# GpSimd adds a fourth tile of gathered rows in a graph kernel; TensorE's products in one run; the last normalisation earlier

## The chip, the cores and the metric

The kernel runs on one core of a Trainium2 chip. The metric is the device time of one execution in microseconds (us), the median of the runs. A core has TensorE (PE in the profile, its weight loads PEld), VectorE (DVE), ScalarE (ACT), GpSimd (POOL) and SyncE (SP), each with its own instruction stream; they wait for each other through semaphores.

## What is computed

Two graph layers over 6250 nodes of 128 features and 100000 edges, each with a residual and a layernorm:

```python
# layer 0 (e: 100000 x 128, fc_w: 512 x 128, attn: 100 x 4 x 128)
f = (e @ fc_w.T).reshape(-1, 4, 128)
w = attn[rel]
feat = sum(leaky_relu(w * f, 0.2), axis=1)
msg = h[src] + feat
x = layernorm(x + segment_sum(msg, dst))
# layer 1
h = x @ W.T + b
s1 = h @ a1_w + a1_b;  s2 = h @ a2_w + a2_b
e = leaky_relu(s1[src] + s2[dst], 0.01)
att = softmax of e over the edges of each src
x = layernorm(x + segment_sum(att * h[dst], src))
```

## The kernel before, in words

The edges are sorted by dst. **Stage 1** (layer 0) takes them in `G0` = 196 groups of 512 edges, four tiles (`TG`) of 128. Per group g, with the engine and the name of the helper:

- SP loads the 512 edge rows (`e_sb`) and relation numbers.
- GpSimd's `group(g)` issues four indirect DMAs (L523), one per tile, which gather the rows x[src] of the group into slot g % 4 of `xg` (printed as `room`). Then `scatter(g - 3)` issues one indirect DMA (L534) that writes sorted edge records. Before the gathers it waits until the slot is free (`agg_done`).
- TensorE's `products(g, u)`, u = 0 to 3: the edge tile times `fc_sb` into FP[u // 2] (L845, float32, two matmul records), and the one-hot relation times the two parts of attn into WP[u % 2] (L854, two records). `aggregate(g - 2)` sums the messages into a 64-column window of nodes: L864 multiplies the four message tiles `msg` with the one-hot `doh`, and L866 multiplies the gathered x rows of the fourth tile with the same `doh` into the same accumulation. `compact(g)` (L877) makes the sorted edge records.
- ScalarE's `step(g)`: `blocks` (L638, `boh`), `copy 0` (L631, WP to `w_sb`), `window_gap` (L648), `copy 1`, `relation` of g + 1 (L618, L623), `copy 2`, `window` (L657, makes `doh`; it overwrites the `doh` of g - 2, so it waits for `agg_done` of g - 2), `copy 3`, `compact` (L665).
- VectorE's `group(g)`: `records` (L1159, `joh`), `weigh_pair` 0 (L1178, z = FP x w_sb for tiles 0 and 1), `halve` and `finish` of g - 1 (L1193 `hs`, L1201 `msg`), `weigh_pair` 1 (L1178, tiles 2 and 3), `accumulate` of g - 2 (L1169, adds AP to `accT`), `add_x` of g - 1 (L1209: adds the x rows of three tiles, `X_DVE` = 3, to `msg`), `slope` (L1185, y = max(0.2 z, z), 2048 elements per partition).

`weigh_pair` 1 of g waits for `copy 3` of g, which stands behind `window` of g on ScalarE. `msg`, `doh`, `joh` have two buffers, `xg` four. FP[0] and FP[1] are each free again when their `weigh_pair` is done.

**Between the stages** the first layernorm and h = x W are computed block by block (52 blocks of 122 nodes).

**Stage 2** (layer 1) takes the edges, now sorted by src block, in at least 200 groups (208 here). GpSimd gathers four tiles of h rows per group (L567, L575); the other engines compute a running softmax sum per block. Once all edges of a block are in, the block is averaged, its residual added, and it is normalised. In the last 16 groups VectorE's `early(j)` does average, residual and statistics of two blocks per group, for blocks 0 to 31 (L1457, L1463, L1468). After the last group (`update`, L1341) come `average`, statistics and `normalise` of the other blocks in runs of 8, 8 and 4, and the normalisation of all 52 (ScalarE L795, VectorE L1517). SP and GpSimd store the output in chunks of eight blocks.

Of the kernel before, what the change touches and what calls it, by code (L numbers as in the profile page):

```python
# [26 lines left out]
EARLY = 32  # L27
RUNS = [(0, EARLY)] + [c for c in CHUNKS if c[0] >= EARLY]
BY_DVE = [q for q in range(NS) if (q % 4 == 3 if q < EARLY else q % 2 == 1)]
# [41 lines left out]
def build(nc, x, x_t, e, src_pg, dst_pg, dst_g, rel_g, fcT, attn, WT, Wn, b, a1, a1b, a2, a2b, out):  # L71
    with ExitStack() as ctx:
# [192 lines left out]
        def sums_of(k):  # L265
# [46 lines left out]
        x_added = sem("x_added")  # L312
        r_done = sem("r_done")
# [23 lines left out]
                     boh_ready, joh_ready, x_added, r_done, r_copied)  # L337
# [51 lines left out]
        n_avg = sem("n_avg")  # L389
        n_stat = sem("n_stat")  # L390
# [122 lines left out]
        def _(pool):  # L513
# [23 lines left out]
            with pool.Fori(0, pass_count(pool)) as p:  # L537
# [4 lines left out]
                for g in range(SLOTS, G0):  # L542
                    group(g, g % SLOTS, False)
                    scatter(g - RLAG, (g - RLAG) % SLOTS, False)
                for j in range(RLAG, 0, -1):
                    scatter(G0 - j, SLOTS - j, False)
                for k in range(SLOTS):
# [51 lines left out]
        def _(act):  # L599
# [173 lines left out]
            with act.Fori(G1_LEAST - 2 * S1, act.snap(more + (G1_LEAST - 2 * S1 + 1)), S1) as i:  # L773
                for k in range(S1):
                    idx(i + k + AHEAD, (k + AHEAD) % S1)
                    block_s1(i + k + AHEAD, (k + AHEAD) % S1, False)
                    step1(i + k, k, False)
            for k in range(S1):
# [3 lines left out]
                step1(tail + k, k, False, k < S1 - 2)  # L782
            for k in range(S1 - 2, S1):
# [4 lines left out]

            for c, (q0, q1) in enumerate(RUNS):
                run = slice(q0, q1)  # L790
                act.wait_ge(n_var, c + 1)
                nc.scalar.activation(rstd[:, run], mv[:, run, 1], ACT.Sqrt, bias=eps_col[0:BN, :]).then_inc(n_std, 1)
                act.wait_ge(n_rs, c + 1)
                for q in [q for q in BY_ACT if q0 <= q < q1]:
                    nc.scalar.activation(xn[:, q, :], xn[:, q, :], ACT.Identity, bias=nmr[:, q:q + 1],  # L795
                                         scale=rstd[:, q:q + 1]).then_inc(fin_act, 1)
# [3 lines left out]
        def _(pe):  # L800
# [185 lines left out]
        def _(dve):  # L986
# [225 lines left out]
            def group(g, k, lead):  # L1212
# [13 lines left out]
            with dve.Fori(0, pass_count(dve)) as p:  # L1226
                for k in range(SLOTS):
                    group(k, k, True)
                for g in range(SLOTS, G0):
                    group(g, g % SLOTS, False)  # L1230
# [219 lines left out]
            def early(j):  # L1450

                if j == 0:
                    dve.wait_ge(st_ready, tail - LAG + 1)
                    weights(0, EARLY)
                if j < S1 * 2:
                    for q in (2 * j, 2 * j + 1):
                        ins = v.scalar_tensor_tensor(xn[:, q, :], o_sb[:, q, 0:P], rstd[:, q:q + 1], xn[:, q, :],  # L1457
# [107 lines left out]
```

## Time and profile before

| | |
|---|---|
| median of 3 runs | 2639.86 us (2639.47 to 2640.49) |
| the profiled execution's own time | 2640.72 us |
| its span | 2638.9 us |
| PE busy | 2162.6 us (82%) |
| DVE busy | 2244.4 us (85%) |
| ACT busy | 1724.0 us (65%) |
| POOL busy | 1914.7 us (73%) |
| stage 1, about | 85 to 1500 us |
| stage 2, about | 1547 to 2608 us, then the end of the last normalisation |

The span is what the engines' records cover; the execution's own time is 1.8 us more. Busy time leaves out semaphore waits, and also the time that GpSimd spends in issuing between two indirect DMAs. Records of one engine may overlap by up to 0.1 us, since an instruction may begin while the one before it still writes; the pace of an engine is therefore read from one start to the next.

### The profile page before, as it was taken

What the parts mean: (1) busy time and instruction counts of PE and PEld (TensorE: products, weight loads), DVE (VectorE), ACT (ScalarE), POOL (GpSimd) and SP (SyncE); (2) the same over time, 40 slices, a digit from 0 to 9 for tenths busy, and PEclk for the clock granted to TensorE, in tenths of its full rate; (3) what the DMA queues carried; (4) which work ended last, traced back from release to release, by engine and by line L of the source; (5) the groups of instructions that cost most, each with busy time, mean ns of one, the idle gap of its engine ahead of it and who ended that gap; (6) DMA issues with size and microseconds to landing.
All of it is one profiled execution on the core that took longest, in us unless ns stands there. A gap on an engine that the chain in (4) does not pass through costs nothing.

```text
span 2638.9 us, 44193 instructions
## 1 busy us (share of the span) xinstructions
PE 2162.6 (82%) x11261; PEld 1540.4 (58%) x11261; DVE 2244.4 (85%) x5690; ACT 1724.0 (65%) x4954; POOL 1914.7 (73%) x1839
## 2 busy tenths in 40 slices
PE   6999999999999999999999746666666666566563
PEld 3566666666666666666666545656566556565553
DVE  8999999999999999999999966666666666666786
ACT  2788888888888888888888544444444444444444
POOL 2377777777777777777777547777777777777772
PEclk8999999999999999999999867676777776877775
DMA  4233333333333333333333233333333333333332
GB/s 132 69 102 106 102 102 103 105 106 103 102 103 105 105 104 102 102 105 104 106 102 103 66 93 80 80 81 79 82 80 81 80 80 82 80 81 81 80 79 61
DMA packets 156597, 244.02 MB, mean 92 GB/s; under 512 B 40836, under 2 KB 84398, under 8 KB 156226
## 3 DMA queue, kind: packets, MB, share of 16 engines
q1 hardware_dynamic: 97730, 132.55, 17.5%
q0 software_dynamic: 58624, 108.72, 17.2%
q8 instruction: 92, 1.51, 0.2%
q14 instruction: 151, 1.24, 0.1%
HBM read 231.99 MB, written 9.12 MB: 91 GB/s over the span
## 4 chain that ended last, share of the span: by engine, by line
DVE 37%; issue 25%; POOL 18%; PE 7%; DMA 6%; DVEq 5%; ACT 1%; POOLq 0%; SPq 0%; ACTq 0%
POOL room L567 17%; DVE y L1185 17%; DVE hs L1193 9%; DMA room<-h_rows,y 5%; DVEq L1165 4%; DVE room L1209 3%; PE FP L935 3%; DVE accT L1169 2%; PE FP L956 1%; PE AP L956 1%; DVE z L1178 1%; DMA room<-h_rows,idx 1%; POOL room L575 1%; DVE joh L1159 1%; DVE arena L1029 1%
## 5 line engine op out<-in xcount | busy, mean ns | idle before, releaser
L523 POOL DMA_INDIRECT room<-in_x,pk x784 | 918.5, 1172 | 289.7 <-issue 276.7
L567 POOL DMA_INDIRECT room<-h_rows,y x756 | 713.5, 944 | 235.1 <-issue 216.2
L845 PE MATMUL FP<-fc_sb,room 128*128 128x512 f32 x1568 | 833.6, 613 | 2.2 <-issue 2.2
L854 PE MATMUL WP<-at_p,rel_oh 100*128 100x512 f32 x1568 | 805.3, 595 | 0.0
L935 PE MATMUL FP<-ident,room 128*128 128x128 f32 x1664 | 340.1, 368 | 387.1 <-DMA room<-h_rows,y 349.0
L631 ACT ACTIVATE w_sb<-WP 128x512 f32<-128x512 f32 x784 | 464.7, 593 | 226.2 <-PE WP L854 220.6
L935 PEld LDWEIGHTS FP<-ident,room 128*128 128x128 f32 x1664 | 289.2, 261 | 434.0 <-DMA room<-h_rows,y 384.1
L854 PEld LDWEIGHTS WP<-at_p,rel_oh 100*128 100x128 f32 x1568 | 298.3, 190 | 377.3 <-issue 377.3
L729 ACT ACTIVATE accT<-accT,neg_big 128x512 f32<-128x512 bf16 x208 | 150.0, 722 | 559.7 <-DVE accT L1331 559.7
L1178 DVE TENSOR_TENSOR z<-FP,w_sb 128x1024 f32<-128x1024 f32 x392 | 478.8, 1221 | 2.8 <-ACT w_sb L631 2.5
L1185 DVE SCALAR_TENSOR_TENSOR y<-z 128x2048 f32<-128x2048 f32 x196 | 452.8, 2310 | 0.0
L845 PEld LDWEIGHTS FP<-fc_sb,room 128*128 128x128 f32 x1568 | 266.7, 190 | 43.4 <-issue 2.6
L748 ACT ACTIVATE room<-room,pr 128x129 f32<-128x129 f32 x832 | 266.6, 392 | 6.8
L534 POOL DMA_INDIRECT sorted_edges<-runs,spot_i x196 | 192.5, 982 | 92.9 <-issue 60.5
L638 ACT ACTIVATE boh<-arena,rank_pay 128x52 f32<-128x52 bf16 x784 | 239.9, 378 | 0.0
L1193 DVE TENSOR_TENSOR hs<-y 128x1024 f32<-128x1024 f32 x196 | 238.4, 1216 | 0.0
L864 PEld LDWEIGHTS AP<-doh,room 128*128 128x128 f32 x1568 | 190.6, 192 | 53.6 <-DVE room L1209 53.6
L864 PE MATMUL AP<-doh,room 128*128 128x64 f32 x1568 | 211.4, 278 | 6.9 <-DVE accT L1169 4.2
L1341 DVE SCALAR_TENSOR_TENSOR arena<-arena,decay,AP 128x129 f32 x104 | 36.1, 347 | 205.6 <-PE AP L956 204.7
L648 ACT ACTIVATE dot<-iota_row,dloc 128x64 bf16<-128x64 f32 x784 | 206.3, 337 | 0.0
L1374 DVE CUSTOM_DVE_ANT_0 hs<-accT,FP 128x512 f32<-128x512 f32 x208 | 141.7, 681 | 17.0 <-PE FP L935 11.7
L1341 DVE SCALAR_TENSOR_TENSOR arena<-arena,decay,FP 128x129 f32 x104 | 35.8, 344 | 125.1 <-PE FP L956 120.3
(241 smaller groups left out, 3151.7 us busy)
## 6 DMA issues: line engine op xcount, KB each, us to landing
room<-in_e SPq DMA_DIRECT2D x196, 256.0 KB, 2.6
rel_sb<-in_rel_g SPq DMA_DIRECT2D x196, 200.0 KB
z<-sorted_sources SPq DMA_DIRECT2D x208, 128.0 KB
room<-in_x,pk POOLq DMA_INDIRECT x784
room<-h_rows,y POOLq DMA_INDIRECT x756
sorted_edges<-runs,spot_i POOLq DMA_INDIRECT x196, 2.0
accT<-in_x_t SPq DMA_DIRECT2D x1, 3125.0 KB, 11.0
h_rows<-arena SPq DMA_DIRECT2D x13, 227.5 KB, 3.0
```

The lines of the kernel that those rows point to most:

```text
L523: pool.indirect_dma_start(xg[:, k, u, 0:P], None, x[:, :], bass.IndirectOffsetOnAxis(ap=pk[:, g, u:u + 1], axis=0)).then_inc(xg_in[k], 16)
L567: pool.indirect_dma_start(hg[k][:, u, :], None, h_dram[:, :], bass.IndirectOffsetOnAxis(ap=sd[:, g * TG + u:g * TG + u + 1], axis=0)).then ...
L631: nc.scalar.activation(w_sb[:, u // 2, u % 2, :], WP[u % 2][:, :], ACT.Copy).then_inc(w_copied, 1)
L638: ins = nc.scalar.activation(boh[:, k % 2, u, :], onehot[:, :, bass.ds(g * TG + u, 1)].rearrange("p b o -> p (b o)"), ACT.Identity, bias=0 ...
L748: nc.scalar.activation(hg[k][:, u, 0:P + 1], hg[k][:, u, 0:P + 1], ACT.Identity, bias=0.0, scale=pr[:, k % 2, u:u + 1]).then_inc(h_scaled, 1)
L845: mm = pe.matmul(FP[u // 2][:, u % 2, :], e_sb[:, k, u, :], fc_sb[:, :], start=True, stop=True)
L854: mm = pe.matmul(WP[u % 2][:, :], rel_oh[:, k % 2, u * P:(u + 1) * P], at_p[:, j, :], start=(j == 0), stop=(j == 1))
L864: pe.matmul(AP_[:, 0:W], msg[:, k % 2, u, :], doh[:, k % 2, u, :], start=(u == 0), stop=False)
L935: mm = pe.matmul(rows_of(k)[:, u * P:(u + 1) * P], hg[k][:, u, P + 1:P + 2].to_broadcast([P, P]), ident[:, :], start=True, stop=True)
L1178: v.tensor_tensor(z[:, h, :, :], FP[h][:, :, :], w_sb[:, h, :, :], ALU.mult).then_inc(z_done, 1)
L1185: v.scalar_tensor_tensor(y[:, :, :, :], z[:, :, :, :], SLOPE0, z[:, :, :, :], ALU.mult, ALU.max).then_inc(y_done, 1)
L1193: v.tensor_tensor(hs[:, :, :], y_all[:, :, 0:D4 // 2], y_all[:, :, D4 // 2:D4], ALU.add).then_inc(hs_done, 1)
```

## The change

In stage 1:

- GpSimd adds the x rows of the fourth tile to `msg` itself (`add_x`, one tensor_tensor of 128 x 128 float32 per group). It stands ahead of the gathers that reuse the slot: GpSimd's `group(g)` first does `add_x(g - 4)`, then waits for VectorE's and its own addition of g - 4, then issues the four gathers. TensorE's product of those rows (L866) goes, and `aggregate` waits for `x_pooled` as well.
- TensorE does the four `products` of a group in one run, then `compact(g)`, then `aggregate(g - 2)`.
- VectorE makes `joh` of g + 1 between `halve` and `finish`, in place of `joh` of g at the start of the group.

In stage 2, `early` starts 48 groups before the end (`TAIL`), takes one block per group for blocks 0 to 43, and computes each block's weight by itself. The normalisation of blocks 0 to 31 is moved into the last eight groups, that of blocks 32 to 43 ahead of the last two updates; blocks 44 to 51 stay behind them.

```diff
-EARLY = 32
-RUNS = [(0, EARLY)] + [c for c in CHUNKS if c[0] >= EARLY]
+RUNS = [(0, 32), (32, 44), (44, NS)]
+EARLY = RUNS[1][1]
+TAIL = 48
...
+            def add_x(g, k):
+                pool.wait_ge(msg_ready, g + 1)
+                pool.wait_ge(xg_in[k], PASS_IN * p + 16 * TG + (g - k) * 16)
+                pool.sem_inc(pool_turn, 1)
+                pool.tensor_tensor(msg[:, k % 2, X_DVE:TG, :], msg[:, k % 2, X_DVE:TG, :], xg[:, k, X_DVE:TG, 0:P],
+                                   ALU.add).then_inc(x_pooled, 1)
+
             def group(g, k, lead):
                 if not lead:
-                    pool.wait_ge(agg_done, g - SLOTS + 1)
+                    add_x(g - SLOTS, k)
+                    pool.wait_ge(x_added, g - SLOTS + 1)
+                    pool.wait_ge(x_pooled, g - SLOTS + 1)
                     pool.sem_inc(pool_turn, 1)
...
             def aggregate(g, k, lead):
                 pe.wait_ge(x_added, g + 1)
+                pe.wait_ge(x_pooled, g + 1)
                 pe.wait_ge(doh_ready, g + 1)
                 if not (lead and k == 0):
                     pe.wait_ge(acc_done, g)
                 for u in range(TG):
-                    pe.matmul(AP_[:, 0:W], msg[:, k % 2, u, :], doh[:, k % 2, u, :], start=(u == 0), stop=False)
-                for u in range(X_DVE, TG):
-                    mm = pe.matmul(AP_[:, 0:W], xg[:, k, u, 0:P], doh[:, k % 2, u, :], start=False,
+                    mm = pe.matmul(AP_[:, 0:W], msg[:, k % 2, u, :], doh[:, k % 2, u, :], start=(u == 0),
                                    stop=(u == TG - 1))
...
             def group(g, k, lead):
-                products(g, k, lead, 0)
-                products(g, k, lead, 1)
+                for u in range(TG):
+                    products(g, k, lead, u)
+                compact(g, k, lead)
                 if not (lead and k < 2):
                     aggregate(g - 2, (k - 2) % SLOTS, lead)
-                products(g, k, lead, 2)
-                products(g, k, lead, 3)
-                compact(g, k, lead)
...
-                records(g, k, lead)
                 weigh_pair(g, k, lead, 0)
                 if prev:
                     halve(*prev)
+                if not last:
+                    records(g + 1, (k + 1) % SLOTS, lead and k < SLOTS - 1)
+                if prev:
                     finish(*prev)
...
-            for j in range(2 * S1):
+            for j in range(TAIL):
                 k = j % S1
-                step1(tail + j, k, False, k, (k - 2) % S1, j < 2 * S1 - 2)
-                early(j)
+                step1(tail + j, k, False, k, (k - 2) % S1, j < TAIL - 2)
+                if j >= 1:
+                    early(j - 1, tail + j)
+                if j == TAIL - 6:
+                    rates(1, slice(*RUNS[0]))
+                    dve.wait_ge(n_rs, 1)
+                if j >= TAIL - 5:
+                    for q in mine[0][2 * (j - TAIL + 5):2 * (j - TAIL + 6)]:
+                        normal(q)
...
+            for j in range(TAIL - LAG, TAIL - 2):
+                update(tail + j, j % S1, False)
+            rates(2, slice(*RUNS[1]))
+            dve.wait_ge(n_rs, 2)
+            for q in mine[1]:
+                normal(q)
+            for j in range(TAIL - 2, TAIL):
                 update(tail + j, j % S1, False)
```

The new `early(i, g)` does, for one block each, the weight of block i, the average with the residual of block i - 1, the statistics of i - 2 and their aggregation for i - 3. On ScalarE, four normalisations (`normal`) stand behind each of the last five groups' steps, and the square roots (`deviations`) behind the last eighth group, the last group, and the last update.

How the order moves is shown at two places. The first is GpSimd in the steady loop of stage 1 (`room<-in_x` is a gather, `sorted_edges` the scatter, `room<-room` the new addition). Before:

```order
L523 DMA room<-in_x,pk 128x128 [waits agg_done]
L523 DMA room<-in_x,pk 128x128 x3
L534 DMA sorted_edges<-runs,spot_i 263808x1 [waits r_copied,sc_in1]
L523 DMA room<-in_x,pk 128x128 [waits agg_done]
L523 DMA room<-in_x,pk 128x128 x3
```

And now:

```order
L525 TENSOR_TENSOR room<-room 128x128 [waits msg_ready,xg_in1]
L535 DMA room<-in_x,pk 128x128 [waits x_added,x_pooled]
L535 DMA room<-in_x,pk 128x128 x3
L546 DMA sorted_edges<-runs,spot_i 263808x1 [waits r_copied,sc_in1]
L525 TENSOR_TENSOR room<-room 128x128 [waits msg_ready,xg_in2]
```

A group has five instructions on GpSimd before, and six now; the first gather now waits for the addition just ahead of it.

The second is TensorE in the same loop (FP and WP are the products, AP the aggregation, EP the compaction). Before:

```order
L845 MATMUL FP<-fc_sb,room 128x512
L854 MATMUL WP<-at_p,rel_oh 128x512 [waits w_copied]
L854 MATMUL WP<-at_p,rel_oh 128x512
L864 MATMUL AP<-doh,room 128x64 [waits acc_done,doh_ready,x_added]
L864 MATMUL AP<-doh,room 128x64 x3
L866 MATMUL AP<-doh,room 128x64
L845 MATMUL FP<-fc_sb,room 128x512 [waits z_done]
```

And now:

```order
L879 MATMUL FP<-fc_sb,room 128x512
L888 MATMUL WP<-at_p,rel_oh 128x512 [waits w_copied]
L888 MATMUL WP<-at_p,rel_oh 128x512
L910 MATMUL EP<-joh,boh 52x32 [waits r_copied,boh_ready,joh_ready]
L910 MATMUL EP<-joh,boh 52x32 x3
L899 MATMUL AP<-doh,room 128x64 [waits doh_ready,acc_done,x_pooled,x_added]
L899 MATMUL AP<-doh,room 128x64 x3
L879 MATMUL FP<-fc_sb,room 128x512 [waits z_done,e_in0]
```

The aggregation moves from the middle of the products to behind the compaction, loses one product, and waits for the addition on GpSimd.

## Rows read from the trace of the kernel before

**Rows 1.** Windows: us; busy of PE, PEld, DVE, ACT, POOL; PEclk; DMA.

```profile
500.00:1000.00 500.00, 500.00 (x2370) 310.25 (x2368) 497.65 (x559) 419.16 (x1116) 393.86 (x349) 1.00 0.35 104
1550.00:2586.00 1036.00, 657.42 (x4088) 603.20 (x4089) 691.37 (x3563) 470.41 (x1650) 783.34 (x830) 0.74 0.36 80
```

**Rows 2.** Timeline of stage 1, DVE: start us, us long, engine line op.

```profile
803.09 2.31 DVE L1185 SCALAR_TENSOR_TENSOR y<-z 128x2048 f32<-128x2048 f32 x1
805.54 1.23 DVE L1178 TENSOR_TENSOR z<-FP,w_sb 128x1024 f32<-128x1024 f32 x1
806.68 1.22 DVE L1193 TENSOR_TENSOR hs<-y 128x1024 f32<-128x1024 f32 x1
807.93 0.69 DVE L1201 TENSOR_TENSOR room<-hs 128x512 f32<-128x512 f32 x1
808.54 1.22 DVE L1178 TENSOR_TENSOR z<-FP,w_sb 128x1024 f32<-128x1024 f32 x1
...
809.80 0.55 DVE L1209 TENSOR_TENSOR room<-room 128x384 f32<-128x384 f32 x1
810.27 2.31 DVE L1185 SCALAR_TENSOR_TENSOR y<-z 128x2048 f32<-128x2048 f32 x1
```

**Rows 3.** The same stretch, POOL: its five instructions of one group.

```profile
803.08 0.98 POOL L523 DMA_INDIRECT room<-in_x,pk  x1 [0.30 <-issue]
804.37 1.86 POOL L523 DMA_INDIRECT room<-in_x,pk  x1 [0.30 <-issue]
...
809.03 0.93 POOL L534 DMA_INDIRECT sorted_edges<-runs,spot_i  x1 [0.30 <-issue]
810.26 0.98 POOL L523 DMA_INDIRECT room<-in_x,pk  x1 [0.30 <-issue]
```

**Rows 4.** Timeline near 103 us and near 179 us, POOL and DVE.

```profile
103.39 1.22 DVE L1193 TENSOR_TENSOR hs<-y 128x1024 f32<-128x1024 f32 x1
103.48 1.94 POOL L523 DMA_INDIRECT room<-in_x,pk  x1 [0.30 <-issue]
```

```profile
179.04 2.29 DVE L1185 SCALAR_TENSOR_TENSOR y<-z 128x2048 f32<-128x2048 f32 x1
179.07 3.08 POOL L523 DMA_INDIRECT room<-in_x,pk  x1 [0.30 <-issue]
```

**Rows 5.** Timeline of stage 1, PE and ACT around the aggregation.

```profile
803.23 0.97 PEld L864 LDWEIGHTS AP<-doh,room 128*128 128x128 f32 x8 [0.25 <-DVE room L1209]
803.25 1.09 PE L864 MATMUL AP<-doh,room 128*128 128x64 f32 x8
...
806.47 0.41 ACT L657 ACTIVATE doh<-dot 128x256 f32<-128x256 bf16 x1
...
807.30 0.60 ACT L631 ACTIVATE w_sb<-WP 128x512 f32<-128x512 f32 x1 [0.42 <-PE WP L854]
```

**Rows 6.** Timeline near 91 us: ScalarE's copy that a scatter waited for.

```profile
91.35 0.19 ACT L665 ACTIVATE runs<-EP 52x32 f32<-52x32 f32 x1
...
92.45 0.92 POOL L534 DMA_INDIRECT sorted_edges<-runs,spot_i  x1 [28.41 <-ACT runs L665]
```

**Rows 7.** Timeline, the instructions of POOL that compute.

```profile
0.26 0.10 POOL L1558 MEMSET const-float32-0.0<- 128x1 f32 x1 [0.26 <-issue]
...
0.87 0.34 POOL L514 IOTA iota_i<- 128x256 int32 x1 [0.40 <-POOLq L1558]
```

```profile
1503.21 5.80 POOL L552 MEMSET arena<- 128x6837 f32 x1 [8.23 <-SPq L467]
```

**Rows 8.** Timeline of the end, DVE and ACT.

```profile
2607.75 0.35 DVE L1341 SCALAR_TENSOR_TENSOR arena<-arena,decay,FP 128x129 f32 x1 [0.65 <-PE FP L956]
...
2612.49 0.64 DVE L1263 BATCH_NORM_AGGREGATE mv<-stats 122x2 f32<-122x6 f32 x8
```

```profile
2629.41 0.28 ACT L792 ACTIVATE rstd<-mv,eps_col 122x4 f32<-122x4 f32 x1
2630.14 0.88 ACT L795 ACTIVATE arena<-arena,nmr,rstd 122x128 f32<-122x128 f32 x2 [0.44 <-DVE nmr L1270]
```

More of the change, by code:

```diff
@@ L26 @@
 CHUNKS = [(q, min(q + 8, NS)) for q in range(0, NS, 8)]
-EARLY = 32
-RUNS = [(0, EARLY)] + [c for c in CHUNKS if c[0] >= EARLY]
-BY_DVE = [q for q in range(NS) if (q % 4 == 3 if q < EARLY else q % 2 == 1)]
+RUNS = [(0, 32), (32, 44), (44, NS)]
+EARLY = RUNS[1][1]
+TAIL = 48
+BY_DVE = [q for q in range(NS) if (q % 4 == 3 if q < RUNS[0][1] else q % 2 == 1)]
 BY_ACT = [q for q in range(NS) if q not in BY_DVE]
@@ L544, in _ @@
                     scatter(g - RLAG, (g - RLAG) % SLOTS, False)
+                add_x(G0 - SLOTS, 0)
                 for j in range(RLAG, 0, -1):
                     scatter(G0 - j, SLOTS - j, False)
+                    add_x(G0 - j, SLOTS - j)
                 for k in range(SLOTS):
@@ L782, in _ @@
                 step1(tail + k, k, False, k < S1 - 2)
+                if k == 0:
+                    deviations(0)
+                if k == 3:
+                    act.wait_ge(n_rs, 1)
+                if k >= 3:
+                    for q in mine[0][4 * (k - 3):4 * (k - 2)]:
+                        normal(q)
             for k in range(S1 - 2, S1):
@@ L786, in _ @@
             decays(tail + (S1 - 1), S1 - 1, False)
[L789 to L796, printed above, removed]
+            deviations(1)
+            for q in mine[0][4 * (S1 - 3):]:
+                normal(q)
+            act.wait_ge(n_rs, 2)
+            for q in mine[1]:
+                normal(q)
+            deviations(2)
+            act.wait_ge(n_rs, 3)
+            for q in mine[2]:
+                normal(q)
         @block.tensor
@@ L1210, in add_x, with group @@
                                 ALU.add).then_inc(x_added, 1)
-            def group(g, k, lead):
+            def group(g, k, lead, last=False):
                 prev = None if lead and k == 0 else (g - 1, (k - 1) % SLOTS, lead)
-                records(g, k, lead)
                 weigh_pair(g, k, lead, 0)
@@ L1229, in _ @@
                 for g in range(SLOTS, G0):
-                    group(g, g % SLOTS, False)
+                    group(g, g % SLOTS, False, g == G0 - 1)
                 halve(G0 - 1, SLOTS - 1, False)
@@ L1472, in _, with normal @@
+            def normal(q):
+                v.tensor_scalar(xn[:, q, :], xn[:, q, :], rstd[:, q:q + 1], nmr[:, q:q + 1], ALU.mult,
+                                ALU.add).then_inc(fin_dve, 1)
+            mine = [[q for q in BY_DVE if q0 <= q < q1] for q0, q1 in RUNS]
             more = group_count(dve)
-            tail = dve.snap(more + (G1_LEAST - 2 * S1))
+            tail = dve.snap(more + (G1_LEAST - TAIL))
             members(0, 0, True)
@@ L1477, in _ @@
                 step1(k, k, True, k, k - 2)
-            for g in range(S1, G1_LEAST - 3 * S1):
+            for g in range(S1, G1_LEAST - TAIL - S1):
                 step1(g, g % S1, False, g % S1, (g - 2) % S1)
-            with dve.Fori(G1_LEAST - 3 * S1, dve.snap(more + (G1_LEAST - 3 * S1 + D1 + 1)), D1) as i:
+            with dve.Fori(G1_LEAST - TAIL - S1, dve.snap(more + (G1_LEAST - TAIL - S1 + D1 + 1)), D1) as i:
                 half = dve.snap(i & (S1 - D1))
@@ L1496, in _ @@
                 spread(*last)
-            early(2 * S1)
-            early(2 * S1 + 1)
-            for j in range(2 * S1 - LAG, 2 * S1):
+            for j in range(TAIL - LAG, TAIL - 2):
+                update(tail + j, j % S1, False)
+            rates(2, slice(*RUNS[1]))
+            dve.wait_ge(n_rs, 2)
+            for q in mine[1]:
+                normal(q)
+            for j in range(TAIL - 2, TAIL):
                 update(tail + j, j % S1, False)
@@ L1510, in average @@
                 moments(q0, q1)
-            def normalise(c):
-                q0, q1 = RUNS[c]
-                rates(c + 1, slice(q0, q1))
-                dve.wait_ge(n_rs, c + 1)
-                for q in [q for q in BY_DVE if q0 <= q < q1]:
-                    v.tensor_scalar(xn[:, q, :], xn[:, q, :], rstd[:, q:q + 1], nmr[:, q:q + 1], ALU.mult,
-                                    ALU.add).then_inc(fin_dve, 1)
-            dve.wait_ge(st_ready, dve.snap(more + G1_LEAST))
-            for c in range(1, len(RUNS)):
-                average(*RUNS[c])
-                normalise(c - 1)
-            normalise(len(RUNS) - 1)
+            dve.wait_ge(st_ready, dve.snap(more + G1_LEAST))
+            average(*RUNS[2])
+            rates(3, slice(*RUNS[2]))
+            dve.wait_ge(n_rs, 3)
+            for q in mine[2]:
+                normal(q)
 def kernel(x, src, dst, edge_attr_128, edge_type_100, L0_gnn_fc_w, L0_gnn_attn, L1_gnn_W, L1_gnn_b, L1_gnn_a1_w,
```

54 lines of the change are left out of this document (33 added, 21 removed).

## Prediction

> **What bounds the kernel now.** I read the page's busy slices, then the windows, then the timeline of one group of stage 1. In the windows [rows 1] DVE is busy 497.65 of 500 us and PE 500.00 in stage 1; in stage 2 neither is, but 830 gathers in 1036 us are one per 1.248 us, the spacing of two gathers that nothing holds up (0.94 us and the 0.30 us of issue), so GpSimd bounds stage 2. In the timeline of stage 1 one `slope` follows the other after 810.27 - 803.09 = 7.18 us [rows 2]. DVE's starts in between leave no hole. So DVE sets the pace, and the question is how much room GpSimd has, which gets the new work.
>
> The page gives POOL as 73% busy, which looks like room. The timeline says otherwise [rows 3]: five instructions per group, and the second gather takes 1.86 us, not 0.94. It begins inside a `slope` (803.09 to 805.40) and ends 804.37 + 1.86 = 806.23, that is 0.83 us after it. The gather at 103.48 begins inside a `halve` (to 104.61) and ends at 105.42, 0.81 us after that [rows 4]. The one at 179.07 begins just behind the start of a `slope`, takes 3.08 us and ends 0.82 us after it [rows 4]. Those that begin inside a z (L1178) keep their 0.94. So **a GpSimd instruction that comes up while DVE runs an operation with both inputs in SBUF is held until that operation is over**; z has FP in PSUM as one input and holds nobody. This fits a rule of the Trainium skill (SBUF — State Buffer, section "SBUF: two separate sides"): DVE and GpSimd share a port pair, and whoever has it keeps it for a whole instruction.
>
> So per group GpSimd needs 5 x 1.25 = 6.25 us and loses 0.92 us to the `slope`: 7.17 us of 7.18. It is as full as DVE. It fits only because one gather starts at the very moment the `slope` does (803.08 and 803.09, again 810.26 and 810.27).
>
> **The added instruction, stage 1.** Its length isn't in the trace. Bounds: a memset of 6837 elements takes 5.80 us, 0.85 ns each, with 0.10 us for a memset of one element, and an iota of 256 takes 0.34 us, 1.3 ns each [rows 7]. One pass of 128 elements by the memset is 0.2 us; three passes (two inputs, one output) by the iota are 0.6 us. Three passes by the memset are 0.10 + 3 x 128 x 0.85 ns = 0.43; I take 0.4 us, since the memset is the longest row and its slope the surest. The Trainium skill (GPSIMD Engine Reference, section "Performance versus the Vector engine") has 4497 ns for 2048 elements of such an add; by that, as an estimate, 128 elements would be about 0.3 us, and the sum 19 us lower. There is also a new wait behind it: the first gather waits for the addition. A scatter that had to wait began 92.45 - 91.54 = 0.91 us after the copy that released it [rows 6], against 0.30 us of plain issue [rows 3]; I keep 0.3 to 0.9.
>
> Even without any hold, 6.25 + 0.4 + 0 to 0.6 is 6.65 to 7.25 us, and the hold of at least 0.9 comes on top. Six instructions don't fit in 7.18 us, so GpSimd falls behind, and the others wait for its additions. The new pace I walk through with the rows, time 0 being the end of an addition:
>
> - PE's aggregation starts within 0.1 of its release and takes 1.09 [rows 5]: 1.15. Now `window` on ScalarE is due, since `doh` is free only then, at 1.20; `copy 3` stands behind it, starts about 0.32 later and takes 0.60 [rows 5]: 2.12. So `weigh_pair` 1 starts at 2.17.
> - DVE by its own intervals [rows 2]: z and accumulate 1.26, add_x 0.47: the `slope` starts at 3.90 and ends at 6.21. z of the next group waits for it (6.25), `halve` at 7.39 to 8.60, handing over at 8.52.
> - GpSimd: gathers at 0.3 to 0.9, then at 1.25 us spacing. The third starts at 2.8 to 3.4, the fourth at 4.05 to 4.65: inside the `slope`. It ends at 6.21 + 0.82 = 7.03. Scatter 7.33 to 8.26. The next addition comes up at 8.3 to 8.5, inside `halve`, gets in at 8.52 and ends at **8.92 us**.
>
> DVE would be ready for its next `weigh_pair` 1 at about 9.3, but must wait until 8.92 + 2.17. The pace is 8.92 instead of 7.18 us: 1.74 us for each of the 192 groups behind the four leading ones, **+334 us**. With the addition at 0.2 or 0.6 us it is 38 us less or more; the length of the wait behind it falls out, since the fourth gather is held to the same moment either way.
>
> **The other parts of stage 1.** The products of L866 go: nothing, since PE already waits 0.25 us per group for DVE [rows 5], and now waits for the addition. The aggregation behind the compaction puts `window` and `copy 3` behind it, and so makes a loop: aggregation 1.1, then at most ScalarE's busy time of a group (419.16 / 500 x 7.18 = 6.0 us [rows 1]) without `copy 2`, 5.4, then the last product on PE, some 0.9: 7.4 us as upper bound. `relation` is in the 6.0 and not in the loop, so I expect under 7.0 and cost it at nothing. It is what is late next if GpSimd isn't, by 0.2 us per group at worst. `joh` moved: it takes 0.21 us between `slope` and z, where z must wait 0.1 us for the `slope` to end anyway, and fills the gap behind `halve` (1.25 instead of 1.14 us to the next start [rows 2]): 0.1 lost, 0.1 won, nothing.
>
> **The end of stage 2.** Before, from the last update's end (2608.10) to the last normalisation's end (2631.02) are 22.9 us [rows 8]. Now only eight blocks are behind it: weights to statistics took 2608.14 to 2613.13 for the same eight-block work [rows 8], the root 0.28, rates and start 0.45, four normalisations on ScalarE 1.7 (two take 0.88): about 7.5 us. That is 15.4 us less. Against it: the moved normalisations, four per group on ScalarE at 0.4 us, mostly lie in its waits (470 of 1036 us busy [rows 1]); I charge 1 us at the last group, 0.5 us for those between the last updates, 1 us for the last two output chunks leaving together, and 1 us for 12 more averages that can hold up a gather for 0.3 us each. DVE's 12 more blocks lie in its idle third. Net **-12 us**, with -5 and -15 as ends.
>
> **Sum** against the profiled execution: 2640.7 + 334 - 12 = 2963 us; the median of the runs is 0.9 us lower: 2962.
>
> **Rivals.**
>
> 1. *One more gather gets in ahead of the `slope`.* If the way from addition to `weigh_pair` 1 takes a little longer, or the wait behind the addition is short, the fourth gather starts in time, the scatter is the one held, and the next addition falls into a z, which doesn't hold it. With 0.3 us behind the addition the fourth gather misses the `slope` by only 0.15 us. Then: scatter held to 6.3 + 0.82 = 7.1, addition 7.3 to 7.7 or 7.8; with the chain 0.7 us longer, 8.3. That is +0.6 to +1.1 us per group, +115 to +215: 2743 to 2842 us. Chance 0.22.
> 2. *The long gather is slack* (other side). If the 0.92 us aren't a loss but room which GpSimd gives up when it has more to do, and the addition is short, six instructions take 6.7 to 7.2 us, DVE stays the bound, and only the end counts: 2640.7 - 12 = 2628 us. It decides as soon as the hold isn't real. Against it speak the 0.81 to 0.83 us behind three different operations [rows 3, 4]. Chance 0.10.
> 3. *The addition fits but holds DVE.* By the same rule of the Trainium skill (same section) a GpSimd instruction that reads SBUF would keep DVE's two-input operations out for its length. No row shows DVE held for long. As a mechanism here: 0.4 us on each of 192 groups, 77 us, and GpSimd not the bound: 2705 us. Chance 0.06.
> 4. *TensorE's clock falls.* PE would be busy 6.7 of 8.9 us, with a hole of about 2 us in each group. In stage 2, busy 657 of 1036 us, the granted clock is 0.74 on average, between the levels of 2.4 and 1.2 GHz, and 1.00 in stage 1 [rows 1]. At 0.75 the 6.7 us are 9.0, and the aggregation, which sits on the path, is longer: 9.2 to 9.8 us per group, 3020 to 3130 us. Chance 0.10.
> 5. *The change does nothing that counts*: the new order cancels out within the measurement. Chance 0.02.
>
> The forecast itself, 8.7 to 9.1 us per group, has 0.50.
>
> **How the numbers follow.** Likeliest: 2962. Its own range is 2915 to 3010. For 8 in 10 the range must take in rival 1 and the lower part of rival 4: 2740 to 3060. About 0.2% (5 us) is what a measurement of this kernel can tell from no change. Faster by more is rival 2, 0.10; within it rival 5, 0.02; slower all the rest, 0.88.
>
> **What would show it.** In the changed profile the stage of 196 groups ends near 1830, not 1500 us; one `slope` follows the other after 8.9 us; DVE has one wait per group of about 1.7 us, at `weigh_pair` 1, put down to ScalarE's `w_sb`, and ScalarE's `doh` waits for AP; POOL shows no long idle time, and one gather of about 3 us in each group that ends 0.8 us behind a `slope`. From the last update to the last normalisation about 8 us. I am wrong if DVE is still without holes in stage 1, or if GpSimd's longest gather stays below 2 us, or if PE's granted clock leaves 1.00 there.

## The result and the profile after

The changed kernel takes **2977.15 us** (median; 2973.43 to 2989.97), the kernel before beside it 2640.18 us (2639.47 to 2640.55). The ratio is 1.1285, with a 95% interval of 1.1272 to 1.1299: slower by 337 us. The forecast was 2962 us.

The first and the last `slope` of stage 1, from the timelines of VectorE, before and after:

```profile
92.80 2.29 DVE L1185 SCALAR_TENSOR_TENSOR y<-z 128x2048 f32<-128x2048 f32 x1
...
1491.91 2.29 DVE L1185 SCALAR_TENSOR_TENSOR y<-z 128x2048 f32<-128x2048 f32 x1
```

```profile
92.67 2.29 DVE L1216 SCALAR_TENSOR_TENSOR y<-z 128x2048 f32<-128x2048 f32 x1
...
1840.15 2.29 DVE L1216 SCALAR_TENSOR_TENSOR y<-z 128x2048 f32<-128x2048 f32 x1
```

Stage 1 is 1747.5 - 1399.1 = 348 us longer, 8.96 us per group instead of 7.17. The span grew by 2971.6 - 2638.9 = 332.7 us. The other 15 us are the end of stage 2. The last `update` ends at 2955.93 and the last normalisation on ScalarE at 2963.41, 7.5 us later, against 22.9 before [rows 8]. Changed kernel, timeline of the end, DVE and ACT:

```profile
2955.58 0.35 DVE L1375 SCALAR_TENSOR_TENSOR arena<-arena,decay,FP 128x129 f32 x1 [0.24 <-DVE arena L1375]
...
2960.31 0.64 DVE L1297 BATCH_NORM_AGGREGATE mv<-stats 122x2 f32<-122x6 f32 x8
```

```profile
2960.99 0.30 ACT L795 ACTIVATE rstd<-mv,eps_col 122x8 f32<-122x8 f32 x1 [4.19 <-DVE mv L1297]
2961.76 1.65 ACT L799 ACTIVATE arena<-arena,nmr,rstd 122x128 f32<-122x128 f32 x4 [0.47 <-DVE nmr L1304]
```

The same window of stage 1 as in [rows 1] (columns as there), and the longest waits in it (engine, line, what it waited for: us, times, longest):

```profile
500.00:1000.00 500.00, 433.11 (x1791) 268.85 (x1791) 408.03 (x446) 323.10 (x890) 385.78 (x335) 0.90 0.28 83
```

```profile
ACT doh L671 <- PE AP L899: 157.4, 55, 4.1
...
POOL room L535 <- issue: 88.1, 198, 0.8
DVE z L1209 <- issue: 81.7, 56, 2.4
```

DVE now has holes, one per group, at `weigh_pair` 1; ScalarE waits for the aggregation. GpSimd's busy time in this window did not rise (385.78 against 393.86 us), though it has a sixth instruction. Per group it did, from 5.6 us (349 instructions, five to a group) to 6.9 (335, six to a group): the groups are longer too. Time in which an instruction is held counts as busy; the waits and the issue time between two instructions don't, so the share shows neither that the engine is full nor why. Two things differ from the forecast. The granted clock is 0.90, not 1.00. And the pace is no constant: of 195 distances between two slopes 45 are 7.5 to 8.0 us, most others 9.0 to 9.9.

One group of 9.3 us, changed kernel, three timelines (as [rows 2], [rows 3] and [rows 5]):

```profile
1002.92 2.28 DVE L1216 SCALAR_TENSOR_TENSOR y<-z 128x2048 f32<-128x2048 f32 x1
1005.33 1.22 DVE L1209 TENSOR_TENSOR z<-FP,w_sb 128x1024 f32<-128x1024 f32 x1
1006.47 1.22 DVE L1224 TENSOR_TENSOR hs<-y 128x1024 f32<-128x1024 f32 x1
1007.61 0.50 DVE L1190 TENSOR_TENSOR joh<-iota_row,rank_pay 128x128 f32<-128x128 f32 x1
...
1010.48 1.23 DVE L1209 TENSOR_TENSOR z<-FP,w_sb 128x1024 f32<-128x1024 f32 x1 [1.77 <-issue]
...
1012.22 2.28 DVE L1216 SCALAR_TENSOR_TENSOR y<-z 128x2048 f32<-128x2048 f32 x1
```

```profile
1004.12 1.90 POOL L535 DMA_INDIRECT room<-in_x,pk  x1 [0.31 <-issue]
1006.32 0.92 POOL L546 DMA_INDIRECT sorted_edges<-runs,spot_i  x1 [0.30 <-issue]
1007.28 0.67 POOL L525 TENSOR_TENSOR room<-room 128x128 f32<-128x128 f32 x1
1008.75 0.98 POOL L535 DMA_INDIRECT room<-in_x,pk  x1 [0.80 <-issue]
...
1012.54 2.78 POOL L535 DMA_INDIRECT room<-in_x,pk  x1 [0.30 <-DVE room L1240]
```

```profile
1003.94 1.02 PE L879 MATMUL FP<-fc_sb,room 128*128 128x512 f32 x2
...
1008.06 1.33 PE L899 MATMUL AP<-doh,room 128*128 128x64 f32 x8 [2.13 <-issue]
1009.19 2.02 PE L879 MATMUL FP<-fc_sb,room 128*128 128x512 f32 x2
...
1009.49 0.42 ACT L671 ACTIVATE doh<-dot 128x256 f32<-128x256 bf16 x1 [3.53 <-PE AP L899]
```

Read from the top: the fourth gather (1004.12) begins inside the `slope` and ends at 1006.02, 0.82 us behind it. The scatter follows. The addition comes up inside `halve` and ends at 1007.95. Only then can the aggregation start (1008.06), then `doh`, `copy 3`, and `weigh_pair` 1 at 1010.48. TensorE has stood still for 2.13 us, and its next pair of products takes 2.02 us instead of 1.02: the granted clock is 0.50 from 1009 to 1011 us, the lower of the two levels, 1.2 GHz, where it was 1.00 up to 1008. The next fourth gather begins at 1012.54 and is held again.

One of the short groups, of 7.53 us, timeline of DVE and POOL:

```profile
159.03 1.18 POOL L535 DMA_INDIRECT room<-in_x,pk  x1 [0.30 <-issue]
159.31 2.29 DVE L1216 SCALAR_TENSOR_TENSOR y<-z 128x2048 f32<-128x2048 f32 x1
160.52 1.88 POOL L546 DMA_INDIRECT sorted_edges<-runs,spot_i  x1 [0.30 <-issue]
161.73 1.23 DVE L1209 TENSOR_TENSOR z<-FP,w_sb 128x1024 f32<-128x1024 f32 x1
162.42 0.42 POOL L525 TENSOR_TENSOR room<-room 128x128 f32<-128x128 f32 x1
...
166.84 2.28 DVE L1216 SCALAR_TENSOR_TENSOR y<-z 128x2048 f32<-128x2048 f32 x1
```

Here the fourth gather begins 0.28 us before the `slope` and gets through in 1.18 us. The scatter is the one held, to 162.40, and the addition falls into z, which doesn't hold it. This is rival 1 as it was described. Of the 191 groups from the fifth `slope` on, the `slope` holds the fourth gather in 117 (median 9.48 us from this `slope` to the next) and the scatter in 73, the 45 short groups among them.

### The profile page after: what moved, and what is told of

Its sections match the earlier page's. It is cut to its first block, busy times and chain, and to the rows that moved or that the text cites. A ratio compares the mean times of both kernels' runs of the same rounds, so it can differ in the third digit from the quotient of the medians.

```text
span 2971.6 us, 44287 instructions
## 1 busy us (share of the span) xinstructions
PE 2285.8 (77%) x10869; PEld 1621.9 (55%) x10869; DVE 2293.8 (77%) x5770; ACT 1684.7 (57%) x4955; POOL 2160.4 (73%) x2035
## 4 chain that ended last, share of the span: by engine, by line
PE 57%; issue 16%; POOL 15%; DMA 5%; DVE 5%; ACT 0%; DVEq 0%; POOLq 0%; SPq 0%; ACTq 0%
PE FP L879 26%; POOL room L581 15%; PE WP L888 13%; PE AP L899 8%; DMA room<-h_rows,y 5%; PE EP L910 3%; PE FP L966 3%; PE FP L987 1%; PE AP L987 1%; DVE arena L1060 0%; DMA room<-h_rows,idx 0%; DVE stats L1319 0%; DVE z L1168 0%; POOL room L589 0%; PE FP L862 0%
## 5 line engine op out<-in xcount | busy, mean ns | idle before, releaser
L535 POOL DMA_INDIRECT room<-in_x,pk x784 | 989.1, 1262 | 379.3 <-issue 348.6
L879 PE MATMUL FP<-fc_sb,room 128*128 128x512 f32 x1568 | 906.3, 661 | 2.2 <-issue 2.2
L888 PE MATMUL WP<-at_p,rel_oh 100*128 100x512 f32 x1568 | 875.5, 642 | 0.0
L966 PE MATMUL FP<-ident,room 128*128 128x128 f32 x1664 | 351.6, 377 | 373.5 <-DMA room<-h_rows,y 340.8
L888 PEld LDWEIGHTS WP<-at_p,rel_oh 100*128 100x128 f32 x1568 | 326.1, 208 | 432.8 <-issue 358.4
L899 PE MATMUL AP<-doh,room 128*128 128x64 f32 x1568 | 257.6, 318 | 245.4 <-issue 238.7
L671 ACT ACTIVATE doh<-dot 128x256 f32<-128x256 bf16 x196 | 81.6, 416 | 556.3 <-PE AP L899 556.3
L899 PEld LDWEIGHTS AP<-doh,room 128*128 128x128 f32 x1568 | 231.5, 227 | 259.7 <-issue 250.8
L879 PEld LDWEIGHTS FP<-fc_sb,room 128*128 128x128 f32 x1568 | 311.5, 212 | 62.3 <-issue 2.6
L546 POOL DMA_INDIRECT sorted_edges<-runs,spot_i x196 | 253.2, 1292 | 90.0 <-issue 58.9
```

Source lines behind the costliest of these rows:

```text
L546: pool.indirect_dma_start(table[:, :], bass.IndirectOffsetOnAxis(ap=spot_i[:, g:g + 1], axis=0), runs[:, k, :], None).then_inc(sc_in[k], 16)
L879: mm = pe.matmul(FP[u // 2][:, u % 2, :], e_sb[:, k, u, :], fc_sb[:, :], start=True, stop=True)
L888: mm = pe.matmul(WP[u % 2][:, :], rel_oh[:, k % 2, u * P:(u + 1) * P], at_p[:, j, :], start=(j == 0), stop=(j == 1))
L899: mm = pe.matmul(AP_[:, 0:W], msg[:, k % 2, u, :], doh[:, k % 2, u, :], start=(u == 0), stop=(u == TG - 1))
L966: mm = pe.matmul(rows_of(k)[:, u * P:(u + 1) * P], hg[k][:, u, P + 1:P + 2].to_broadcast([P, P]), ident[:, :], start=True, stop=True)
```

## The experiments

Theory A is the walk of the prediction: GpSimd's sixth instruction makes the fourth gather meet the `slope`, and the hold sets the pace. The rivals: the other edits (order, `joh`), and TensorE's clock. All edits are against the changed kernel unless said otherwise. The first four runs and the next four were each timed beside the kernel before, at 2639.65 and 2639.09 us.

**1. Without the addition.** GpSimd's `add_x` and its waits go, TensorE multiplies the fourth tile's x rows again. The other edits stay.

```diff
-                    add_x(g - SLOTS, k)
-                    pool.wait_ge(x_added, g - SLOTS + 1)
-                    pool.wait_ge(x_pooled, g - SLOTS + 1)
+                    pool.wait_ge(agg_done, g - SLOTS + 1)
```

> The changed kernel without GpSimd's addition: TensorE multiplies the fourth tile's x rows again, all else as changed (products in one run, joh moved, new end of stage 2). Theory A (GpSimd has no room for a sixth instruction): stage 1 is back at 7.18 us per group, the total at 2640 less the 15 us of the end, 2625 us, within 5. Rival B (the new order on TensorE makes ScalarE's window and copy 3 late and sets the pace): the pace stays above 7.5 us and the total above 2690 us.

2636.75 us, ratio to before 0.9988 (0.9978 to 0.9997), 7.23 us per group. The addition with its wait is the whole loss, 340 us. But the total was to be 2625 us within 5, and 12 us are missing.

**2. The new end alone.** The kernel before with the new end of stage 2 and nothing else (edit 1, TensorE's products two and two again, `records(g)` at the start of VectorE's group).

> The kernel before with the new end of stage 2 alone. Both theories: 15 us less than before, 2625 us. Beside the first run it prices the new order on TensorE and VectorE: under A the two are within 5 us of each other; under B this one is clearly faster.

2624.95 us, ratio 0.9945 (0.9928 to 0.9962): faster than both kernels, 15 us at the end as seen above. It is the best version of this study. So the two reorderings of stage 1 cost the 12 us, 0.06 us per group. VectorE's timeline with them (run 1) and without (run 2):

```profile
801.36 2.28 DVE L1206 SCALAR_TENSOR_TENSOR y<-z 128x2048 f32<-128x2048 f32 x1
803.77 1.23 DVE L1199 TENSOR_TENSOR z<-FP,w_sb 128x1024 f32<-128x1024 f32 x1
...
806.04 0.30 DVE L1180 TENSOR_TENSOR joh<-iota_row,rank_pay 128x128 f32<-128x128 f32 x1
806.26 0.68 DVE L1222 TENSOR_TENSOR room<-hs 128x512 f32<-128x512 f32 x1
```

```profile
801.45 2.32 DVE L1208 SCALAR_TENSOR_TENSOR y<-z 128x2048 f32<-128x2048 f32 x1
803.70 0.28 DVE L1182 TENSOR_TENSOR joh<-iota_row,rank_pay 128x128 f32<-128x128 f32 x1
803.90 1.23 DVE L1201 TENSOR_TENSOR z<-FP,w_sb 128x1024 f32<-128x1024 f32 x1
...
806.30 0.69 DVE L1224 TENSOR_TENSOR room<-hs 128x512 f32<-128x512 f32 x1
```

From `slope` to z 2.41 us against 2.45, from z to `finish` 2.49 against 2.40: the sum is 4.90 against 4.85, in this one group. `joh` between `slope` and z cost almost nothing, since z waits for the end of the `slope` in the kernel (`y_done`); behind `halve` it costs more than it fills.

**3. The addition in the old order.** The addition stays; TensorE's products are two and two around the aggregation, as before, and `joh` is in its old place.

```diff
-                for u in range(TG):
-                    products(g, k, lead, u)
-                compact(g, k, lead)
+                products(g, k, lead, 0)
+                products(g, k, lead, 1)
                 if not (lead and k < 2):
                     aggregate(g - 2, (k - 2) % SLOTS, lead)
+                products(g, k, lead, 2)
+                products(g, k, lead, 3)
+                compact(g, k, lead)
```

> GpSimd's addition in the old order of TensorE and VectorE (aggregation between the second and third product, joh at the start of the group), new end of stage 2. Theory A: GpSimd still has six instructions and a slope to sit out, 8.9 us per group or up to 0.5 off, total 2870 to 3050 us. Rival B: the pace is near 7.2 us and the total under 2660 us.

3104.28 us (3099.65 and 3108.91), more than I expected. Its waits from 500 to 1000 us:

```profile
ACT w_sb L645 <- PE WP L888: 182.6, 144, 5.8
...
DVE z L1211 <- ACT w_sb L645: 109.8, 29, 5.9
...
POOL room L535 <- DVE room L1242: 47.3, 21, 3.1
```

An aggregation that waits for GpSimd now stands ahead of two products. So `copy 2` and `copy 3` are late, VectorE waits for them, and GpSimd in turn waits for VectorE's own addition: a circle through four engines. The pace is no constant here either: 82 groups of 7.0 to 7.2 us stand between others, nearly all of 8.9 to 13.3 us. The new order of stage 1 keeps the loss down to 337 us; by these waits it is the four products in one run that do it, though `joh` was moved back as well and isn't taken apart here.

**4. The `slope` in two halves.** If holds by the long `slope` set the pace, two instructions of half the length must give much of it back.

```diff
+                for h in range(2):
+                    ins = v.scalar_tensor_tensor(y[:, h, :, :], z[:, h, :, :], SLOPE0, z[:, h, :, :], ALU.mult, ALU.max)
+                ins.then_inc(y_done, 1)
```

> The changed kernel with VectorE's slope as two instructions of 1024 elements in place of one of 2048; same work. Theory A (a GpSimd instruction is held until the running operation with two inputs in SBUF ends): the longest hold is halved, a GpSimd instruction gets in between the halves, the pace falls to 7.8 to 8.4 us and the total to 2740 to 2870 us. If the hold is not the cause, VectorE only pays a second start, some 0.06 us per group, and the total stays at 2975 to 2990 us.

2726.43 us (2708.25 and 2744.62, so far apart that the size is rough), most groups 7.5 to 7.6 us in the profiled run of 2708.25 us, clock 1.00. The addition with all its waits is still there, and 251 of the 337 us are gone. This is the strongest evidence for the hold. It even went below my range: GpSimd's addition now gets in between the halves, in 174 of 196 groups.

**5. The addition behind the gathers.** `add_x(g - 3)` goes behind the gathers of g, so that no gather waits for an addition just ahead of it.

```diff
-                    add_x(g - SLOTS, k)
                     pool.wait_ge(x_added, g - SLOTS + 1)
...
                     group(g, g % SLOTS, False)
+                    add_x(g - RLAG, (g - RLAG) % SLOTS)
                     scatter(g - RLAG, (g - RLAG) % SLOTS, False)
```

> The changed kernel with GpSimd's addition of g - 3 behind the four gathers of g (ahead of the scatter), so that the wait for it is over when the next gathers come up. Theory A (what counts is the slope that GpSimd has to sit out): the 0.5 us of extra wait only moves the fourth gather's arrival inside the slope, total unchanged, 2977 within 40 us. Theory C (the exposed wait behind the addition is what costs): 0.5 us less for each of 192 groups, 2880 us.

2890.08 us (2888.39 and 2891.77), 87 us less than the changed kernel; A's expectation missed. Mean 8.54 us per group: 96 groups of 7.1 to 8.1 us, the others 9.0 to 10.4. Theory C's 2880 us is 10 us off, but it had 0.5 us less in each group, and that is not what the groups show.

**6. Both, 4 and 5.**

> The same late addition with the slope in two halves. There the long holds are gone (7.55 us per group, all of it GpSimd's own: 0.6 + 0.8 + 1.4 + 4 x 1.25 less small change), so the 0.5 us of wait are on the path: theory A gives 7.1 to 7.35 us per group, total 2640 to 2680 us. If the pace there is set by something else than GpSimd's sum, it stays at 2708 us.

2697.85 us (2696.72 and 2698.98), and a uniform 7.54 us: above my range. From 500 to 1000 us, and one group of DVE and POOL:

```profile
500.00:1000.00 500.00, 485.79 (x2120) 284.98 (x2118) 491.19 (x597) 382.33 (x1061) 404.49 (x399) 1.00 0.35 98
```

```profile
801.72 2.56 DVE L1217 SCALAR_TENSOR_TENSOR y<-z 128x1024 f32<-128x1024 f32 x2
804.42 1.23 DVE L1209 TENSOR_TENSOR z<-FP,w_sb 128x1024 f32<-128x1024 f32 x1
```

```profile
802.64 0.56 POOL L525 TENSOR_TENSOR room<-room 128x128 f32<-128x128 f32 x1
803.39 1.71 POOL L545 DMA_INDIRECT sorted_edges<-runs,spot_i  x1 [0.19 <-issue]
```

VectorE is without holes again. The addition runs at the seam of the halves (802.64 to 803.20), and the pair takes 2.56 us where one `slope` took 2.28. From `slope` to z are 2.70 instead of 2.41 us. Run 1's 7.23 us plus 0.29 are 7.52: VectorE's own sum, lengthened by the halving and by the addition's hold, sets the pace here, not GpSimd's. The halving is 0.07 us of it and the hold 0.22: the pairs without an addition in them take 2.35 us.

**7. TensorE kept busy.** Four products of 128 x 128 ahead of each aggregation's wait, into a part of PSUM that nobody reads; they compute for nothing. The wait for `acc_done` goes ahead of them.

```diff
+                for _ in range(4):
+                    pe.matmul(AP_[:, 128:256], ident[:, :], ones[:, :], start=True, stop=True)
                 pe.wait_ge(x_added, g + 1)
```

> The changed kernel with four extra 128x128 float32 products on TensorE ahead of each aggregation, into unused columns of AP, so that it idles some 1.1 us less per group; they are computed for nothing. If the granted clock (0.90 in stage 1 of the changed kernel) stretches the path from addition to weigh_pair 1, it is back near 1.00 and the pace of the slow groups falls from 9.0 to 9.9 to about 8.9 us; where more groups then catch the slope is open: total 2930 to 2980. If the clock plays no part: same time, or later by what the filler adds.

2987.90 us (2986.16 and 2989.64), granted clock 1.00 from 500 to 1000 us, and nearly all groups at 9.0 or 9.1 us. One group, POOL and DVE:

```profile
1006.24 0.67 POOL L525 TENSOR_TENSOR room<-room 128x128 f32<-128x128 f32 x1
1007.72 0.98 POOL L535 DMA_INDIRECT room<-in_x,pk  x1 [0.81 <-issue]
...
1011.51 2.51 POOL L535 DMA_INDIRECT room<-in_x,pk  x1 [0.30 <-issue]
```

```profile
1009.18 1.23 DVE L1211 TENSOR_TENSOR z<-FP,w_sb 128x1024 f32<-128x1024 f32 x1 [1.52 <-issue]
...
1010.92 2.28 DVE L1218 SCALAR_TENSOR_TENSOR y<-z 128x2048 f32<-128x2048 f32 x1
```

The addition ends at 1006.91. Counted from there, `weigh_pair` 1 starts at 2.27, the `slope` at 4.01, the fourth gather at 4.60, and the gather ends at 7.11. The walk had 2.17, 3.90, 4.05 to 4.65, and 7.03. With the clock at 1.00 the loop is the one I walked. In 188 of 191 groups the `slope` holds the fourth gather. Without the filler there are groups of 9.9 and of 7.5 us, and the whole is 11 us faster: the falling clock costs nothing on balance.

**8. The addition of one element.** GpSimd adds 1 element per partition instead of 128; 127 of the 128 x columns of the fourth tile are left out of the sum.

```diff
-                pool.tensor_tensor(msg[:, k % 2, X_DVE:TG, :], msg[:, k % 2, X_DVE:TG, :], xg[:, k, X_DVE:TG, 0:P],
-                                   ALU.add).then_inc(x_pooled, 1)
+                pool.tensor_tensor(msg[:, k % 2, X_DVE:TG, 0:1], msg[:, k % 2, X_DVE:TG, 0:1],
+                                   xg[:, k, X_DVE:TG, 0:1], ALU.add).then_inc(x_pooled, 1)
```

> The changed kernel with GpSimd's addition cut to one element per partition (left out of the sum: the other 127 x columns of the fourth tile). Same instructions, waits and holds, the length from 0.40 to about 0.1 us. Theory A (a sixth instruction, whatever its length): 0.3 us less per group, -55 us, still above 2850 us. Rival D (the length of the addition is the cost): most of the 337 us go, total under 2750 us.

2920.26 us (2918.93 and 2921.60), 57 us less. The 127 elements are a sixth of the 340 us. The rest is that there is an instruction with a wait on each side, whatever its length.

**9, 10 and 12. Which reordering costs the 12 us?** Run 9 is run 2 with `joh` moved, run 10 is run 2 with TensorE's new order; run 12 repeats run 9.

> The kernel before with the new end of stage 2 and joh moved behind halve; TensorE in its old order, no addition on GpSimd. It splits the 12 us (0.067 us per group) that the two reorderings cost together (2636.75 against 2624.95 us). Theory J: the joh move costs it. Where joh of the group stood between slope and z, z's 0.1 us of waiting for the slope's end lay under it; now z waits for that end in the open (2.41 us from slope to z, against 2.23 + 0.21), and joh costs its whole 0.3 us behind halve where there was no wait to cover. Then 2635 to 2639 us here. Theory O: TensorE's order costs it, VectorE waiting for FP or w_sb a little in each group. Then 2623 to 2627 us here. I lean to J, 2 to 1.

> The kernel before with the new end of stage 2 and TensorE's four products in one run with the aggregation behind the compaction; joh in its old place, no addition on GpSimd. Theory J (the joh move costs the 12 us): 2623 to 2627 us. Theory O (TensorE's order costs them): 2635 to 2639 us. Granted clock 1.00 and 7.15 to 7.25 us per group by both.

> The same kernel as in the run with joh moved alone (the kernel before, the new end of stage 2, joh behind halve). In that call even the kernel before took 3065 us, so the totals there decide nothing between J (the joh move costs the 12 us) and O (TensorE's order does). In the groups there that nothing disturbed the slope-to-slope time was 7.24 us, against 7.17 without the move and 7.23 with both. Theory J: 2635 to 2639 us where the kernel before takes about 2640, and 7.23 us from slope to slope. Theory O: 2623 to 2627 us and 7.17 us. Now 5 to 1 for J.

Inconclusive. These ran on other chips, on which the kernel before took 3065.41 us (runs 9 to 11) and 3085.32 us (run 12). Run 9 shows what differs: its stage 2 issues 655 gathers in 1000 us where the changed kernel above issues 802, at a granted clock of 0.62 instead of 0.72, and its stage 1 has groups of 8.2 to 9.7 us between groups of 7.2. GpSimd itself isn't slower: two gathers still follow each other after 1.25 us, but 102 times in stage 2 the next one comes only after 2.0 us or more, mostly up to 4.4, and 68 of these waits the profile puts down to no engine and no DMA of this core ("remote"). What it is stays open. Run 9 took 2994.66 us (0.9778, 0.9735 to 0.982), run 12 2998.98 (0.9724, 0.969 to 0.9758), run 10 3049.39 (0.9951, 0.9928 to 0.9973); these say nothing of 12 us at 2640. Beside the kernel before on the same chip run 10 is 16 us faster, as much as the new end alone gives, and runs 9 and 12 are 71 and 86 us faster: there the move of `joh` seems to gain, not to cost. Stage 1 takes 1519.8 us in run 9 and 1569.8 in run 10; why, no run here shows. The groups that nothing disturbed do say a little: the medians of those under 7.3 us are 7.24 us (run 9, 120 groups), 7.25 (run 12, 120), 7.20 (run 10, 93), against 7.17 in run 2 and 7.23 in run 1. That points to `joh` for most of it, as run 1's timeline does. It isn't settled.

**11. Runs 5 and 7 together.**

> The changed kernel with the addition made one group later, behind the gathers (as in the run with 2890 us), and with four products of 128 x 128 in each group on TensorE that nobody uses, which kept the granted clock at 1.00 in the run with 2988 us. It tells what saved the 87 us. Theory S (the chips clock did it: with a slower aggregation path the slope comes later and the fourth gather gets in ahead of it in a part of the groups): with the clock at 1.00 the pace is uniform, 8.8 to 9.0 us, and the time 2950 to 2990 us. Theory W (the wait between addition and first gather did it, 0.5 us shorter, which lets the gathers get in ahead): the fast groups stay or become more, 2800 to 2900 us. My walk with time 0 at the addition says that without the wait the fourth gather starts 0.3 us before the slope only if the first one starts within 0.15 us, so I lean to W, 3 to 2.

3207.45 us (3206.99 and 3207.91), ratio 1.0471 (1.0413 to 1.0529) to those 3065.41 us, so the total can't be held against the expectations. Its stage 1 can: the granted clock is 1.00, stage 1 takes 1729.7 us from first to last `slope` (run 5: 1665.3; run 7: 1760.2), and it runs in two clean patterns. Timelines of POOL near 200 us and near 1000 us:

```profile
203.29 0.42 POOL L525 TENSOR_TENSOR room<-room 128x128 f32<-128x128 f32 x1
...
205.35 1.93 POOL L534 DMA_INDIRECT room<-in_x,pk  x1 [0.30 <-issue]
...
211.06 0.42 POOL L525 TENSOR_TENSOR room<-room 128x128 f32<-128x128 f32 x1
```

```profile
999.37 0.68 POOL L525 TENSOR_TENSOR room<-room 128x128 f32<-128x128 f32 x1
...
1004.44 2.71 POOL L534 DMA_INDIRECT room<-in_x,pk  x1 [0.30 <-DVE room L1242]
...
1008.42 0.67 POOL L525 TENSOR_TENSOR room<-room 128x128 f32<-128x128 f32 x1
```

The first 24 groups repeat every 7.8 us: the first gather meets the second half of a `slope` and takes 1.93 us, and nothing else is held for long. Then comes a longer group, the third gather meets the start of a `slope` and takes 2.71 us, the addition falls into `halve` (0.67), and from there the pattern of 9.0 us repeats itself to the end but for a few groups. It is as long as that of run 7. So at the full clock the loop without the wait between addition and gather is as slow as with it, once it has fallen into the slow pattern. Theory S foresaw that, where I had leaned to W. By it, what run 5 gained came with the falling clock, which moves the `slope` against the gathers from group to group. This fits, but it isn't shown: on this chip stage 1 is disturbed in run 9 and run 10 too, which have no addition, and run 11 may have fallen into the slow pattern by such a disturbance.

## Why the prediction was right, and where it was not

- **GpSimd as full as DVE, the long gather a loss.** Right. Run 4 halves the `slope`, and with it the longest hold, changes nothing else, and gives 251 of 337 us back. Rival 2 (the long gather is slack) is out.
- **The length of the addition.** 0.40 us taken, 0.41 to 0.42 measured where nothing holds it (77 times in the changed kernel), 0.67 to 0.69 when it comes up in `halve` (116 times). The estimate from a figure of the Trainium skill (GPSIMD Engine Reference, section "Performance versus the Vector engine") was some 0.3 us; the trace has 0.41 and decides. The wait behind it was bounded by 0.3 and 0.9 and is 0.80. Six instructions without any hold are then 0.80 + 4 x 1.25 + 0.97 + 0.41 = 7.18 us: they fit only if nothing is ever held.
- **The walk, 8.92 us.** Right in mechanism: step by step in run 7 (9.03 us), where the addition takes 0.67 us as `halve` holds it, and each step is up to 0.1 us later. That the changed kernel's mean is as close (8.96) is luck: its 49 groups under 8.1 us have a mean of 7.62, the 146 others one of 9.41, and the forecast had neither. The short ones save 64 us against 8.92, the long ones lose 72. As a term, +334 us forecast, 340 measured (run 1 and the changed kernel).
- **"The length of the wait behind it falls out".** Wrong as it stands. Run 5, with that wait gone from the way to the first gather, gains 87 us; it moves the addition too, so the wait's length isn't tested alone. The step held for the one pattern that I walked; I took it that the loop has only one. It has at least two, of 7.8 and 9.0 us (run 11). The faster is of the size of rival 1, priced at 7.8 to 8.3 us. In the changed kernel the `slope` holds the scatter, as in rival 1, in 73 of 191 groups, and the fourth gather, as in the forecast, in 117. So the two weren't alternatives for the whole stage: they occur in turn.
- **`joh` and TensorE's order at nothing.** Wrong by 12 us (runs 1 and 2). I had said for `joh` "0.1 lost, 0.1 won"; run 1 and run 2 show that less was won than lost. In the changed kernel itself `joh` costs more yet, 0.50 us in 117 groups.
- **TensorE's clock.** I gave "leaves 1.00" as a sign against me, and rival 4 a price of 60 to 170 us. The clock did fall, to 0.90, right behind the hole of 2 us. Where the fourth gather is held, the price was about right too: a median of 9.48 us per group, where rival 4 had 9.2 to 9.8 and run 7, at 1.00, has 9.05. From the end of the addition to `weigh_pair` 1 it is 2.53 us in the group above and 2.27 in run 7; the aggregation takes 1.33 instead of 1.09 us [rows 5]. But run 7 as a whole is no faster, since at 1.00 it has no more than five groups under 8.1 us. That the falling clock is what makes the short groups is argued from run 7 alone, whose filler also adds work and moves a wait. By my own sign the forecast should have failed; the total held because the two effects cancel.
- **The addition holds DVE (rival 3).** Not as the main cost, but it is real: `joh` takes 0.50 us when it meets the addition, 0.28 otherwise, and in run 6 the seam of the halves shows it. This is the rule of the Trainium skill (SBUF — State Buffer, section "SBUF: two separate sides") seen from the other side: whichever of the two starts first keeps the shared ports for its whole instruction. The trace agrees, with 0.22 us in both cases.
- **The end of stage 2.** -12 us forecast, -15 measured (22.9 - 7.5 = 15.4): the 3.5 us that I charged for work moved under others cost nothing. The 7.5 us of the new end was exact.

Together: the addition 340 us instead of 334, the reorderings 12 instead of 0, the end -15 instead of -12. These are the 15 us by which 2977 lies above 2962.

## What to carry to other kernels

An engine's busy share doesn't say how much room it has: count its instructions per group, add the issue time, and look how each one stands to the long two-input instructions of VectorE. A small piece of work moved to GpSimd costs its count, its waits and its place in time; here the work itself was a sixth of the cost (run 8). When a loop of engines is this full, walk it through once, but ask also whether it has a second pattern that repeats itself, and which disturbance tips it from one to the other.

## What I had not expected of the hardware

- Indirect DMAs of GpSimd are held by VectorE's operations with both inputs in SBUF until these end, and complete 0.80 to 0.87 us after (the gathers of the kernel before and of the changed kernel). With the `slope` in two halves (run 4) all but 9 of 768 gathers take 1.3 us or less.
- TensorE's products take 2.02 us a pair instead of 1.02 right behind a hole of 2.13 us, and are back at 1.02 about 4 us later (changed kernel, from 1009.19 and from 1013.32 us); with four small products in each group ahead of the aggregation's wait the granted clock stays at 1.00 (run 7).
- The kernel before took 2639 us on the chips of runs 1 to 8, and 3065 and 3085 us on those of runs 9 to 12. Whether the chip itself is the reason isn't shown. A few microseconds can only be read beside the kernel before on the same chip, and not on every chip.
